# Key product behind the last score tile, high keys behind the last exponential, scatters spread over four steps, more prologue fillers

## The reference

```python
mod = (_silu(c) @ wmod).reshape(B, 6, 1, -1)          # sa, ca, ga, sb, cb, gb
h = _layernorm(x) * (1 + ca) + sa
q, k, v = einsum('bsx,xAnh->Abnsh', h, w);  q = q + q_bias
a = q @ k.T * 64 ** -0.5                              # per batch and head, 512 x 512
emb = einsum('sf,fnh->nsh', sins, positional)
a = softmax(where(tril, a + relative_causal(q @ emb.T * 64 ** -0.5), -1e9))
x = x + ga * ((a @ v) @ out_kernel + out_bias)
h = _layernorm(x) * (1 + cb) + sb
score = softmax(h @ Wg + bg); gate, idx = max(score), argmax(score)
buf[idx, pos] = h             # pos: running count of the expert, dropped from 256 on
out = relu(buf @ W1 + b1) @ W2 + b2
x = x + gb * out[idx, pos] * gate
```

## Time and profile before

| | |
|---|---|
| runs | 935.09 us median of 3 (935.01 to 935.53) |
| the profiled execution: its own time | 937.85 us |
| its span | 935.7 us |
| PE, DVE, ACT, POOL busy | 884.9, 701.6, 664.4, 584.4 us |
| DMA moved | 56.01 MB, mean 60 GB/s |

### The profile page before, as it was taken

How to read it: one execution, slowest core, us unless ns; L and a number is a source line. 1 busy time by engine, 2 the same in 40 slices (tenths; PEclk the granted TensorE clock), 3 DMA queues, 4 the chain that set the end, 5 groups by cost and what they waited for, 6 DMA issues and landing times. The chain is left out here.

```text
span 935.7 us, 18012 instructions
## 1 busy us (share of the span) xinstructions
PE 884.9 (95%) x5515; PEld 676.6 (72%) x5515; DVE 701.6 (75%) x2115; ACT 664.4 (71%) x1843; POOL 584.4 (62%) x917
## 2 busy tenths in 40 slices
PE   7799999999999999999999999999999999998994
PEld 6666777777777777777777767777677777666994
DVE  3678778787887778787878787877877777853784
ACT  3587777877778777877787778777787777750551
POOL 3365655777557766667577765776676757553354
PEclk7799999999999999999999999999999999999998
DMA  7223332112010111011100111010101110005671
GB/s 285 57 80 91 91 86 57 46 46 69 18 37 24 49 32 38 19 40 41 43 23 23 48 33 28 19 42 23 43 18 29 34 43 23 24 16 194 221 219 42
DMA packets 36513, 56.01 MB, mean 60 GB/s; under 512 B 7447, under 2 KB 21512, under 8 KB 36161
## 3 DMA queue, kind: packets, MB, share of 16 engines
q1 hardware_dynamic: 32624, 46.16, 17.5%
q0 software_dynamic: 3072, 5.94, 1.8%
q10 hardware_dynamic: 720, 2.75, 0.9%
HBM read 23.96 MB, written 16.82 MB: 44 GB/s over the span
## 5 line engine op out<-in xcount | busy, mean ns | idle before, releaser
L612 ACT ACTIVATE prob<-srow,nmax 128x512 f32<-128x512 f32 (+3 forms) x512 | 286.2, 559 | 150.6 <-DVE nmax L1167 147.7
L1167 DVE CUSTOM_DVE_ANT_0 srow<-bank,consts 128x512 f32<-128x512 f32 (+3 forms) x512 | 247.0, 488 | 111.1 <-issue 98.3
L454 POOL TENSOR_SCALAR prob<-prob,rsum 128x128 f32<-128x128 f32 (+3 forms) x512 | 263.3, 532 | 46.7 <-DVE rsum L1179 45.1
L845 PE MATMUL bank<-consts,prob 128*128 128x128 f32 x1280 | 201.8, 272 | 0.4 <-POOL prob L454 0.2
L621 ACT ACTIVATE pt<-bank 128x384 f32<-128x384 f32 x318 | 159.5, 502 | 22.2 <-PE bank L845 18.0
L845 PEld LDWEIGHTS bank<-consts,prob 128*128 128x128 f32 x1280 | 158.4, 141 | 23.0 <-POOL prob L454 1.1
L835 PE MATMUL bank<-khi,qhi 128*128 128x512 f32 (+2 forms) x384 | 158.2, 412 | 15.9 <-POOL qlo L447 13.2
L445 POOL CAST qhi<-qx 128x384 fp32r<-128x384 f32 x128 | 68.3, 534 | 167.4 <-PE bank L835 115.9
L865 PE MATMUL bank<-pt,v 128*64 128x512 f32 (+3 forms) x1024 | 152.0, 439 | 0.1
L447 POOL TENSOR_TENSOR qlo<-qx,qhi 128x384 fp32r<-128x384 f32 x128 | 128.9, 1007 | 10.8
L1206 DVE SCALAR_TENSOR_TENSOR klo<-bank,khi 64x512 fp32r<-64x512 f32 x128 | 88.0, 687 | 58.1 <-ACT kx L579 56.1
(11 more groups left out here) (193 smaller groups left out, 1475.5 us busy)
## 6 DMA issues: line engine op xcount, KB each, us to landing
qx<-g SPq DMA_DIRECT2D x252, 64.0 KB, 2.0
xbuf<-fill SPq DMA_DIRECT2D x16, 385.0 KB, 4.3
x<-xbuf SPq DMA_DIRECT2D x16, 385.0 KB, 3.6
raw<-in_w SPq DMA_DIRECT2D x16, 256.0 KB, 3.0
prob<-in_w SPq DMA_DIRECT2D x16, 256.0 KB, 4.3
out<-row SPq DMA_DIRECT2D x8, 256.0 KB, 2.6
x<-in_x SPq DMA_DIRECT2D x1, 1792.0 KB, 14.9
modb<-mod_rows SPq DMA_DIRECT2D x8, 192.0 KB, 3.7
```

The source lines that it names most:

```text
L454: end = gp.tensor_scalar(part, part, rsum[:, par, 4 * h + q:4 * h + q + 1], 1.0, ALU.mult, ALU.mult)
L612: act.activation(prob[:, par, h, QOFF[q]:QOFF[q] + P * (q + 1)], srow[:, k % 4, 0:P * (q + 1)], ACT.Exp, bias=nmax[:, par, k:k + 1], scale ...
L845: last = pe.transpose(out[:, n * P:(n + 1) * P], prob[:, par, h, QOFF[q] + k * P:QOFF[q] + (k + 1) * P], ident)
L1167: dve.tensor_tensor_reduce(out=srow[:, k % 4, 0:w], in0=scb[k % 2][:, 0:w], in1=mask[:, S - w:S], scale=-1.0, scalar=BIG, op0=ALU.add, op1 ...
```

## The change

The diff has four parts.

1. PE: `project_k` moves from behind tile 6 to behind tile 7 (in step 0 also behind that step's own value product), ahead of `project_g` and `weighted`.
2. ACT: the high keys of head 0 move from between exponentials 6 and 7 to behind exponential 7, where those of head 1 follow at once.
3. POOL: a batch's four scatters stand one each at a = 6, a = 7 and a = 0 and 1 of the next turn. In the last turn a = 6 and 7 keep two each. The wait for the landing, which stood ahead of the second division of a = 7, stands at a = 1 of the next turn.
4. PE: `idle(16)` becomes `idle(40)`.

```diff
-                        if a == 6:
-                            scatter(b, (0, 1))
-                        if a == 7:
-                            scatter(b, (2, 3))
+                        if a >= 6:
+                            scatter(b, (2 * a - 12, 2 * a - 11) if last else (a - 6,))
+                    if b > 1 and a < 2:
+                        scatter(b - 1, (a + 2,))
...
-                    divide(j, a % 2, 1, *([("scat", 64 * b)] if a == 7 and not first else []))
+                    divide(j, a % 2, 1, *([("scat", 64 * b - 64)] if a == 1 and b > 1 else []))
...
-                    if after and k == 6:
-                        evac_k(j + 1, 0)
                     if k == 6 and a == 4 and not first:
                         gates(b)
                 if after:
-                    evac_k(j + 1, 1)
+                    for h in range(2):
+                        evac_k(j + 1, h)
...
-            idle(16)
+            idle(40)
...
-                    if k == 6 and after:
+                    if not before:
+                        first_step(k)
+                    if k == 7 and after:
                         if first and a in (0, 3):
                             pe.wait_ge(s["kwh"], 1 if a == 0 else 2)
                             pe.wait_ge(s["kwl"], 1 if a == 0 else 2)
                         pe.wait_ge(s["qe"], 2 * j + 4)
                         project_k(j + 1, n, m)
-                    if not before:
-                        first_step(k)
```

## The result

The changed kernel takes 973.09 us (median of 4 runs, 970.07 to 974.01), the kernel before 935.05 (4 runs): 1.040 times as long, 95% interval 1.0376 to 1.0425. It was forecast at 975, with 964 to 985 for 8 in 10.

What follows compares the result with a forecast made beforehand. PE was taken to bound the kernel, with low keys binding some odd step ends. Loop +44.4, fillers -4 and scatters 0 gave +40.4 on 935.1, so 975 us, range 964 to 985.

Steps and rivals of the forecast that it cites:

- The product behind tile 7: Step end on PE: DVE holds tile 7 in place, so the moved key product is uncovered, 0.70 us in most steps.
- The high keys behind exponential 7: ACT: high keys and low keys come 0.51 us later; a = 3 and 5 pay 0.51, a = 1 0.86.
- 0.68 later: Step end at a = 4: low keys end 1.09 us later, so the next tile 0 starts 0.68 us later.
- about 0.2 late: DVE at a = 4: position product reads follow the low keys, so DVE reaches the next tile 0 0.2 us late.
- the 44.4: Loop total: 5.56 us a batch over eight batches, corrected for the first batch, last batch and last step.
- about 1.0: First batch: weight splits on DVE ahead of the last tiles add about 1.0 us.
- Rival (E): Step starts wait for POOL's queue, hiding PE's product; fewer scatters gain, about 925 to 930 us; chance 0.03.
- Rival (B): Later high keys on ACT cost nothing and odd step ends swallow PE's 0.70 us: 955 us; chance 0.06.
- Rival (D): DVE's step-end work is late in other steps than a = 4 too: about 988 us; chance 0.05.
- I take the middle, -4: Prologue: 24 more fillers close PE's pause and may keep its clock up, 0 to -6 us, taken as -4.
- Rival (C): Idle in each step drops PE's clock for stretches of the loop: over 1030 us; chance 0.04.
- PE's clock below 1.00 in the loop: Sign in the changed trace that the forecast is wrong; it expected clock 1.00 through the loop.

Runs made afterwards that it cites:

- the scatters alone: The kernel before with only the scatter move, one scatter a step over four steps: 933.92 us, ratio 1.0000.
- early keys: The kernel before with 40 fillers and head 0's high keys ahead of exponential 6 at a = 3, 5: 0.9914; with a = 1 and residual sum behind low keys: 0.9866.
- the ACT part alone: The kernel before with only head 0's high keys moved behind exponential 7: 954.35 us, ratio 1.0201.
- the fillers alone: The kernel before with only 40 fillers in place of 16: 933.6 us, ratio 0.9994.

## Why the prediction was right

**The product behind tile 7.** Right in mechanism and size: 0.67 to 0.72 at a = 0, 2, 6 and 7 alone, 0.69 to 0.70 with the rest. That DVE's order holds tile 7 in place was the step that decided it, and the earlier trace rows had it: 56 such waits, short ones, which the product had kept short. They grew to 60.9 us; the forecast said some 60. The idle ahead of tile 7 was read as 1.13 us and is 0.97, which changes nothing in the sum, since the product is uncovered either way.

**The high keys behind exponential 7.** Right in mechanism, too dear: "One exponential occupies ACT for 0.50 us ... for the sum 0.51" took the 256-column exponential for the 128-column one, which occupies it for about 0.40. That lowers a = 3 from 0.51 to 0.38 and, with exponential 7 starting 0.06 sooner than worked out (2.37 us behind tile 7, not 2.43), a = 1 from 0.86 to 0.70. At a = 4 "0.68 later" became 0.50. DVE's "about 0.2 late" became about 0.1: its tile 0 starts 1.20 us behind PE's there instead of 1.10, and this shows one step on, at a = 5, as a tile 7 that comes 0.08 later; with the keys' 0.40 that is its 0.47. So 5.56 a batch was 4.8, and from tile 0 of step 0 to that of step 63 the 44.4 became 37.8: 4.5 us less than forecast in batches 1 to 6, 1.5 less in batch 0, where the "about 1.0" more did not come (at the full clock step 0 pays nothing, 14.28 us against 14.30), and 0.6 less in batch 7.

**Reading past the label.** The view of the kernel before named POOL's `qlo` for 26 starts of a step. Reading its end against that of `klo` led to the low keys, and four runs bear it out: the scatters alone change nothing, early keys gain 0.9% and 1.3%, and later keys cost 2.0%. Rival (E) falls with that. Rival (B) falls with the ACT part alone. Rival (D) did not come: DVE's reads after `klo` stayed inside their cover at all places but a = 4, and there cost some 0.1 us.

**The fillers.** "If the clock then stays at its upper level ... I take the middle, -4" was the wrong term: alone it measures 0.9994, 0 within 2 us. It took one execution's clock for the kernel's. The cost of the lower clock was sized rightly: "about 2.8 us earlier" and "about 3 us more at most" are the 2.9 and 3.0 us that the profiles differ by. But a run with 16 fillers need not pay it, and the changed kernel with 40 paid 2.3 us of it in step 0. The clock of the changed kernel's prologue did stay up to 22 us, and fell in the next pause. That error of +4 and the loop's error of -6.6 went against each other, and the sum of 975 is nearer to 973.1 than its terms deserve: that part is luck.

**The clock in the loop.** Rival (C) did not come as priced: 1.00 over 700 us with 1 us of idle in every step. It came in the first two steps only, for 2.3 and 0.7 us; "PE's clock below 1.00 in the loop" had been named as a sign of being wrong, and it is one for steps 0 and 1 of this execution.

**The tail.** From tile 0 of step 63 the changed kernel took 1.6 us longer in its profiled execution, for which the forecast had nothing. The attention's last step is the same to 0.02 us; the difference lies in the experts. The twelve profiles, all with the same experts, differ there by 1.9 us (113.2, the kernel before itself, to 115.1 with the fillers alone), so it is not put down to the change. PE waits there for the load of `x` from `xbuf` for 1.1 us in the changed kernel's profile and not at all in that of before; but the 114.6 of the scatters alone have no such wait either, and the 113.5 of early keys at a = 3 and 5 have 1.7 us of it. The mean clock of the stretch (0.93 to 0.97) does not order them either. What makes it vary stays open.

## What to carry to other kernels

A product that stands between two waits of its engine for another engine may be free only there: before moving it, ask which of the two waits comes last by the other engine's own order, and what else could fill the gap. When two engines both hold the next step's start, a step pays the larger delay, so price the change step by step and not by adding its parts. A pause or a clock read from one execution's prologue may be that execution's alone; look at a second one before giving it a price.

## What was not expected of the hardware

The same prologue with 16 fillers ran with PE at 1.2 GHz from 16 to 33 us behind an idle of 2.82 us in one execution, and at 2.4 GHz until 21.6 us behind one of 2.69 in another; the idle of 1.65 us ahead of tile 0 of step 0 was followed by the lower clock in the changed kernel and not in the profile of the scatters alone. While the clock stood at 0.50 in the kernel before, PE was busy for 14.60 of 16.30 us. The runs of the kernel before spread over 6.4 us (931.82 to 938.18). With PE kept busy in both pauses they spread over 3.3. And a loop step of the changed kernel, step 1, lost the full clock for a stretch after idles of 0.57 and 0.98 us, which at later places, in steps of the same form, were followed by no fall, nor in the same step of the changed kernel with 16 fillers (idle 0.98, and the weighted sum in 2.38 us instead of 3.63):

```profile
47.00:49.30 2.30, 1.22 (x7) 0.97 (x8) 2.20 (x8) 1.81 (x5) 1.98 (x4) 1.00 0.00 0
49.30:52.70 3.40, 3.40 (x11) 1.12 (x11) 2.20 (x8) 2.31 (x8) 2.43 (x4) 0.50 0.32 77
52.70:56.00 3.30, 3.30 (x26) 2.58 (x23) 1.47 (x5) 1.32 (x4) 2.84 (x6) 0.99 0.83 241
```
